# A transformer kernel of six blocks: attention products of two chunks interleaved, first feed-forward reordered, ring of 6 state buffers, relu(k) from PSUM

## The reference

```python
def _L0_attn_ref(...):        # stage 0, first half: linear attention, 16 heads
    qp, kp = elu(q) + 1, elu(k) + 1
    kv = einsum('bhsd,bhse->bhde', kp, v)
    z = einsum('bhsd,bhd->bhs', qp, kp.sum(axis=2))[..., None]
    attn = einsum('bhsd,bhde->bhse', qp, kv) / (z + EPS)
def _L0_xattn_ref(...):       # stage 0, second half: selective scan, 16 states, gated by z = x
    dA = exp(d[..., None] * A)
    state = state * dA + (d * u)[..., None] * b[:, None, :]
    y = einsum('bdn,bn->bd', state, c)
def _L0_ffn_ref(x, w_fc, w_proj):             # stage 1, inner width 1280
    # ternarize_weight: q in {-1, 0, 1} by a threshold of 0.7 * mean(|w|), times mean(|w|)
    h = square(relu(x @ ternarize_weight(w_fc).T))
    return h @ ternarize_weight(w_proj).T
def _L1_attn_ref(x, weight_qkv, weight_proj): # stage 2: causal, over the 4 batch entries
    qkv = x.reshape(-1, hidden) @ weight_qkv.T    # 16 query heads, 4 key/value heads of 32
    probs = softmax(where(causal, q @ k.T * scale, -inf))
    return (probs @ v) @ weight_proj.T
# stage 3: cross-attention, 16 heads of 128; stage 4: gated feed-forward with looked-up weights
x = layernorm(x + block(x))                   # after each of the six blocks
```

## Time and profile before

| | us |
|---|---|
| median of 3 runs (lowest, highest) | 3073.07 (3070.09, 3076.58) |
| profiled execution, its own time | 3069.51 |
| its span | 3067.8 |
| stage 0 in the span | 0 to about 880 |
| preparing stage 1 | about 880 to 909 |
| stage 1 | about 909 to 1107 |
| stage 2 | about 1117 to 1328 |
| stages 3 and 4 | the rest |

### The profile page before, as it was taken

The page is one execution under the profiler, slowest core; times in us unless marked ns, Lnnn a source line. Parts: engine busy times, 40 slices in busy tenths (PEclk is TensorE's granted clock), DMA queues, the critical chain, the costliest instruction groups (busy, mean ns, idle before and its releaser), DMA issues.

```text
span 3067.8 us, 29404 instructions
## 1 busy us (share of the span) xinstructions
PE 2742.9 (89%) x8882; PEld 1498.7 (49%) x8882; DVE 2002.3 (65%) x3924; ACT 1104.3 (36%) x2014; POOL 643.8 (21%) x569
## 2 busy tenths in 40 slices
PE   6788888788748877889999999999999999899998
PEld 2323333333326654445554555455544555478886
DVE  3996987988974436568782888278855788233222
ACT  4335335344322311135541555145532555221111
POOL 0542543525510024521111111011101111000000
PEclk9998998998979989999999999999999999999999
DMA  3111111101120121310002000200012001400000
GB/s 116 55 48 49 55 49 55 61 35 63 48 110 28 41 75 46 140 36 15 18 26 81 15 18 18 82 26 14 18 43 64 18 15 39 160 28 28 28 14 14
DMA packets 67391, 145.10 MB, mean 47 GB/s; under 512 B 8115, under 2 KB 24755, under 8 KB 66230
## 3 DMA queue, kind: packets, MB, share of 16 engines
q1 hardware_dynamic: 56310, 106.15, 10.6%
q0 software_dynamic: 5472, 21.01, 1.8%
q10 hardware_dynamic: 5472, 16.32, 1.5%
HBM read 113.77 MB, written 29.69 MB: 47 GB/s over the span
## 4 chain that ended last, share of the span: by engine, by line
PE 57%; DVE 25%; issue 10%; POOL 3%; ACT 2%; DMA 2%; DVEq 1%; SPq 1%; POOLq 0%; ACTq 0%
PE bank L474 32%; DVE h L1156 8%; PE bank L758 7%; PE bank L713 3%; PE bank L772 3%; PE bank L773 3%; PE bank L776 3%; DVE sm L1388 2%; DVE p L1399 1%; DVE val L1327 1%; PE bank L801 1%; PE bank L698 1%; PE bank L802 1%; PE bank L803 1%; DVE val L1335 1%
## 5 line engine op out<-in xcount | busy, mean ns | idle before, releaser
L1465 POOL TENSOR_TENSOR h<-du,Bb 128x1024 f32<-128x1024 f32 x128 | 308.7, 2418 | 220.9 <-DVE h L1161 131.5
L883 ACT ACTIVATE bank<-dt,A 128x512 f32<-128x512 f32 x256 | 176.8, 691 | 379.9 <-DVE h L1156 379.8
L1156 DVE TENSOR_TENSOR_SCAN h<-bank,h 128x512 f32<-128x512 f32 x256 | 297.8, 1203 | 15.3 <-POOL h L1465 15.1
L1005 ACT ACTIVATE p<-bank,sm,rq 128x512 f32<-128x512 f32 x256 | 199.0, 777 | 208.1 <-DVE sm L1392 208.1
L594 PE MATMUL bank<-h,ident 128*128 128x512 f32 x256 | 155.2, 690 | 100.7 <-DVE h L1161 100.6
L474 PE MATMUL bank<-pT,v 128*128 128x512 f32 x512 | 232.9, 598 | 3.1 <-ACT pT L828 3.1
L191 POOL TENSOR_SCALAR rstd<-mv 128x1 f32<-128x1 f32 x96 | 28.4, 295 | 981.3 <-DVE mv L185 981.3
L474 PE MATMUL bank<-xT,wxq 128*128 128x512 f32 x512 | 230.6, 593 | 3.2 <-ACT xT L828 3.2
L758 PE MATMUL bank<-woh,oT 128*128 128x512 f32 x512 | 224.4, 600 | 8.6 <-DMA woh<-in_Wo 6.6
L1520 POOL TENSOR_TENSOR rq<-rq,mhalf 128x4 f32<-128x4 f32 x64 | 65.5, 1024 | 790.8 <-DVE rq L1379 790.8
L474 PE MATMUL bank<-kr,q 128*128 128x512 f32 x512 | 230.6, 593 | 0.0
(11 more groups left out here) (199 smaller groups left out, 5085.0 us busy)
## 6 DMA issues: line engine op xcount, KB each, us to landing
Bb<-bc_dram SPq DMA_DIRECT2D x32, 512.0 KB, 3.6
Cb<-bc_dram SPq DMA_DIRECT2D x32, 512.0 KB, 3.8
x_dram<-xo POOLq DMA_DIRECT2D x16, 1024.0 KB, 4.7
xc<-x_dram SPq DMA_DIRECT2D x16, 1024.0 KB, 5.2
woh<-in_Wo SPq DMA_DIRECT2D x64, 256.0 KB, 2.7
idx<-in_idx SPq DMA_DIRECT2D x64, 129.0 KB, 2.1
w_dram<-val SPq DMA_DIRECT2D x64, 129.0 KB, 2.4
xc<-in_x SPq DMA_DIRECT2D x4, 1024.0 KB, 7.9
```

The costliest lines, as they stand in the source:

```text
L883: act.activation(bank[2 + n][:, :], dt[:, et, :], ACT.Exp, scale=A[:, et, 2 * w + n:2 * w + n + 1]).then_inc(dA_ready, 1)
L1005: act.activation(p4[:, t, :], bank[4 + t][:, :], ACT.Exp, bias=sm4[:, 4 + t:5 + t], scale=rq[:, hh % 2, 1, t:t + 1], accum_out=sm4[:, 8 + ...
L1156: dve.tensor_tensor_scan(h[:, s, n, :], bank[2 + n][:, :], h[:, s, n, :], 0.0, ALU.mult, ALU.add).then_inc(scanned, 1)
L1465: pool.tensor_tensor(h[:, U % HR, :, :], du[:, et:et + 1, :].to_broadcast([P, 2, S]), Bb[:, w % 2, :, :], ALU.mult).then_inc(dBu_ready, 1)
```

## The change

- `HR` goes from 4 to 6, so `input_of(U)` waits for PE's addition of unit U - 6 and, as before, for DVE's unit U - 3.
- relu(k) is no longer made by ACT: `exp_min` has two activations, and DVE takes max(k, 0) from the PSUM bank in the same instruction that adds the exponential. So PE may write over a key's bank only after DVE has read it (`key_consumed`), which stands ahead of keys 2 and 3 and of values 0 and 1.
- Stage 1: SP loads `w1` late in stage 0 and `w2` and x of chunk 0 as soon as their places are free; ACT sums both weights; x of chunk 0 is turned ahead of that and split between DVE's two halves of `q1`; PE starts with `q1` alone. In the loop, x of the next chunk is turned between the inner products and those down, and split ahead of the norms; the products down wait for the hidden tiles one by one.
- Stage 2: `qkv` has two buffers. While chunk c is attended, PE turns x of chunk c + 1 and makes its q, k, v between the output products; the orders of ACT, DVE and POOL are interleaved to match, with the norms of chunk c between the scores of chunk c + 1.
- The loops of stages 1 and 2 are written out on PE, ACT, DVE and SP, and stage 2's on POOL too.

```diff
-HR = 4
+HR = 6
-        qkv = s3("qkv", [P, B, QKV])
+        qkv = s3("qkv", [P, 2, B, QKV])
...
             if stages >= 2:
-                sp.wait_ge(stored, STORED0 + 16 * B)
-                simple_stage(1, rows_of)
+                sp.wait_ge(a_full, START + A0[0] + after(B - 1, PER_A[0], 24))
+                sp.dma_start(w1[:], io["w_fc"]...).then_inc(fc_loaded, 16)
+                sp.wait_ge(ln_sum, START + after(B, 8, -4))
+                weights(1, w2, io["w_proj"])
+                for c in range(B):
+                    load_chunk(1, c, c % 2, rows_of)
...
+                    def key_consumed(j):
+                        pe.wait_ge(qk_ready, START + after(c, KD + NT, KD + j + 1))
...
                         if U in (0, 1):
+                            key_consumed(U)
                             project(wk, U + 2, 16, 0)
+                        if U in (3, 4):
+                            key_consumed(U - 1)
                         if U in (3, 4, 6, 7):
                             project(wv, (U - 3) // 3 * 2 + U % 3, 20, 1)
...
+                pe.wait_ge(ln_sum, START + T0[1])
+                turn1(0)
                 pe.wait_ge(abs_sum, START + 2)
                 group(bank[6][:, 0:2], [(ones[:, :], am[:, 0, 0:2])], abs_all)
-                pe.wait_ge(tern, START + 2)
-                        turn(1, c, 0, xc[:, p], x_loaded[p], x_count(1, i))
-                        pe.wait_ge(x_split, START + after(c, KD, KD))
...
-                        pe.wait_ge(h_ready, START + after(c, KF0, KF0))
+                pe.wait_ge(tern, START + 1)
+                for c in range(B):
+                    inner(c)
+                    if c + 1 < B:
+                        turn1(c + 1)
+                    if c == 0:
+                        pe.wait_ge(tern, START + 2)
+                    down1(c)
...
+                turn2(0)
+                for b in range(B):
+                    project2(0, b)
+                for c in range(B):
+                    turn_attended(c, 0)
+                    if c + 1 < B:
+                        turn2(c + 1)
+                    out2(c, 0)
+                    for b in range(1, B):
+                        turn_attended(c, b)
+                        if c + 1 < B:
+                            project2(c + 1, b - 1)
+                        out2(c, b)
+                    if c + 1 < B:
+                        project2(c + 1, B - 1)
...
+                    def exp_min(j, k):
+                        d = filled(0, c, k)
+                        act.activation(er[:, j % 2, 0, :], d[:, :], ACT.Relu, scale=-1.0).then_inc(neg_ready, 1)
+                        act.activation(er[:, j % 2, 0, :], er[:, j % 2, 0, :], ACT.Exp, scale=-1.0).then_inc(a_done, 1)
...
+                act.wait_ge(fc_loaded, START + 16)
+                act.activation(wabs[:, :], w1..., ACT.Abs, accum_out=am[:, 0, 0:1]).then_inc(abs_sum, 1)
...
+                for c in range(B):                      # ACT, stage 2
+                    turned(c, 0)
+                    if c + 1 < B:
+                        x_turned(c + 1)
+                    turned(c, 1)
+                    exps(c, 3)
+                    if c + 1 < B:
+                        projected(c + 1, 0)
+                    turned(c, 2)
...
+                            dve.scalar_tensor_tensor(kp[:, j - KD, :], bank[j % 2][:, :], 0.0, er[:, j % 2, 0, :],
+                                                     ALU.max, ALU.add).then_inc(qk_ready, 1)
...
+                        attend(c, 2)                    # DVE, stage 2, for each c
+                        scores(c, 3)
+                        first(0)
+                        attend(c, 3)
                         dve.wait_ge(stored, STORED0 + 32 * B + 16 * c)
+                        last(0)
+                        scores(c + 1, 0)                # these only if c + 1 < B
+                        first(1)
+                        attend(c + 1, 0)
+                        last(1)
+                        scores(c + 1, 1)
+                        first(2)
+                        attend(c + 1, 1)
+                        last(2)
+                        scores(c + 1, 2)
+                        first(3)
+                        last(3)
```

More of the change, by code:

```diff
@@ L605, in _, with turn1, inner, down1 @@
             if stages >= 2:
+                def turn1(c):
+                    turn(1, c, 0, xc[:, c % 2], x_loaded[c % 2], x_count(1, c // 2))
+                def inner(c):
+                    pe.wait_ge(x_split, START + after(c, KD, KD))
+                    for f in range(KF0):
+                        d = a_bank(1, c, 4 + f)
+                        group(d[:, :], [(q1[:, k, f * P:(f + 1) * P], x[:, k, :]) for k in range(KD) for x in (x_hi, x_lo)], a_full)
+                def down1(c):
+                    for t in range(NT):
+                        pe.wait_ge(ln_sum, START + T0[1] + after(c, 4, t + 1 - 4))
+                        for f in range(KF0):
+                            if t == 0:
+                                pe.wait_ge(h_ready, START + after(c, KF0, f + 1))
+                            pe.matmul(bank[4 + t][:, :], h_hi[:, f, t * P:(t + 1) * P], q2[:, f, :], start=(f == 0), stop=False)
+                            m = pe.matmul(bank[4 + t][:, :], h_lo[:, f, t * P:(t + 1) * P], q2[:, f, :], start=False, stop=(f == KF0 - 1))
+                        m.then_inc(v_full, 1)
@@ new lines, in filled3, with x_turned, projected @@
+                def filled3(*name):
+                    return filled(2, 0, TILES3[name])
+                def x_turned(c):
+                    for k in range(KD):
+                        d = filled3("x", c, k)
+                        bring(xT[:, k, :], d[:, :])
+                def projected(c, b):
+                    if c >= 2 and b == 0:
+                        act.wait_ge(at_first, START + after(c - 1, B, 0))
+                        act.wait_ge(at_added, START + after(c - 1, ADDS, 0))
+                    for n in range(2):
+                        d = filled3("qkv", c, b, n)
+                        bring(qkv[:, c % 2, b, n * QKV // 2:(n + 1) * QKV // 2], d[:, 0:QKV // 2])
@@ new lines, in exps, with turned @@
+                def exps(c, b):
+                    s = sce[:, b * H0:(b + 1) * H0, 0:b + 1]
+                    act.wait_ge(sm_sub, START + after(c, B, b + 1))
+                    act.activation(s, s, ACT.Exp, scale=float(HD) ** -0.5).then_inc(sm_exp, 1)
+                def turned(c, b):
+                    d = filled3("at", c, b)
+                    bring(at3T[:, :, b * P:(b + 1) * P], d[:, :].rearrange("p (k s) -> p k s", k=KD))
+                x_turned(0)
+                act.wait_ge(ln_sum, START + T0[2])
@@ L1207, in _, with x_rest @@
             if stages >= 2:
-                dve.wait_ge(stage_loaded[1], START + L0[1])
-                dve.tensor_reduce(am[:, 0, 0:1], w1[:, :, :].rearrange("p k n -> p (k n)"), AX.X, ALU.add,
-                                  apply_absolute_value=True).then_inc(abs_sum, 1)
+                def x_rest(c):
+                    for k in range(KD):
+                        dve.wait_ge(a_done, START + A0[1] + after(c, PER_A[1], k + 1))
+                        dve.tensor_tensor(x_lo[:, k, :], bank[k][:, :], x_hi[:, k, :], ALU.subtract).then_inc(x_split, 1)
                 dve.wait_ge(abs_all, START + 1)
@@ L1249, in _, with scores @@
                 dve.wait_ge(stage_loaded[2], START + L0[2])
-                with dve.Fori(0, B // 2) as i:
-                    for p in range(2):
-                        c = 2 * i + p
-                        def scores(b):
+                for c in range(B):
+                    for p in (c % 2,):
+                        def scores(c, b):
                             s = sc[:, b * H0:(b + 1) * H0, 0:b + 1]
```

277 lines of the change are left out of this document (153 added, 124 removed).

## The result

The kernel after the change takes 3002.69 us by the median of its runs (2997.80 to 3006.79). The kernel before, timed beside it, takes 3074.82. The ratio is 0.9764, with a 95% interval of 0.9744 to 0.9783: 72 us are gone.

A forecast was written before the change was run, and what follows sets the result against it. Bounds: stage 0 mostly DVE, with a PE backlog; preparation weights' load and DVE; stage 1 PE; stage 2 three engines, none full. 0 - 15.4 - 34.9 - 25 = -75.3 from 3069.5 gives 2994.2 profiled, forecast 2996; range 2970 to 3018.

The forecast's parts named there:

- Stage 0, 0 predicted: Stage 0: at most 40 us of collisions could go, but the new key wait takes most back; net 0, bounds +8 and -40.
- the backlog: Stage 0, units 0 to 10: PE lags behind, so value tiles come late and POOL, held by PE's additions, meets DVE's multiplications.
- Whatever the ring does: Stage 0: DVE's unit 11 starts at 553.7 against 554.97, a gain of 1.3 us a chunk regardless of the ring.
- The loss at U = 30: Stage 0: with six slots POOL starts 2 us earlier and meets DVE's multiplication; about 1.1 us lost.
- Its price for relu(k) from PSUM: Stage 0, keys' additions: 0.74 us with a bank against 0.69, 0.8 us in all, hidden under PE's backlog.
- Preparing stage 1, -15.4 predicted: Before stage 1: earlier weight loads let PE start at 894.0 instead of 909.4; bounds -10 and -18.
- Stage 1, -34.9 predicted: Stage 1: 193.4 us falls to 158.5 as waits and six cold starts go; bounds -28 and -37.
- Stage 2, -25 predicted: Stage 2: last output product at T = 177 instead of 202, T counted from 1121.70; bounds -9 and -36.
- x is never late: Rival, stage 2: DVE runs ahead, so PE never waits for x; 10 us more gained, 2986; chance 0.10.
- DVE and POOL bound stage 2: Rival: port collisions keep the period at 46, stage 2 gives 9 us, 3012; chance 0.18 together with no early loads.
- The ring does what it looks made for: Rival, stage 0: POOL falls in step with DVE, up to 40 us of collisions go; at three quarters 2966; chance 0.13.
- Slower: Rival, stage 0: the wait for key 0 starves the scan; decides from 19 us a chunk; chance 0.01.

The follow-up runs named there:

- e2: Kernel after the change with the ring back at 4, so stage 0 keeps only relu(k) from PSUM with its wait; ratio 0.9800.
- e3: Kernel after the change with the ring back at 4 and relu(k) made by ACT again, without the wait; 3002.1 us, ratio 0.9753.
- e1: Kernel after the change with relu(k) made by ACT again, without the wait for the keys; the ring of 6 stays; ratio 0.9692.
- e7: Kernel after the change, but PE waits for both weights before stage 1's first inner product; 3009.73 us, ratio 0.9788.
- e4: Kernel after the change, but DVE reads key 0 ahead of unit 0 and key 1 ahead of unit 1; 2982.5 us, ratio 0.9693.
- e8: e4 with PE's loop of stage 0 written out besides; 2977.6 us, ratio 0.9687.
- e6: Kernel after the change with a third buffer of x, used in stage 2 only; ratio 0.9763.

## Why the prediction was right

It said 2996 us and 2970 to 3018; 3002.69 was measured, 6.7 more.

- **Stage 0, 0 predicted, +2.6.** The account up to unit 11 held to 0.8 us, and so did the conclusion that the backlog takes back what the ring gives. Two of its sentences were wrong. "Whatever the ring does" is refuted by e2: without the ring the same edit costs 19.5 us, because POOL is then held by PE's additions. And the collisions did not stay at 3.1 to 3.3 (which "units 7 to 13" overstates: only units 7, 8 and 10 had them). They shrank to 1.5 to 1.9, and the time became a wait for ACT. The loss at U = 30, put at 1.1 us, was 0.5: units 24 to 31 of chunk 2 took 35.9 us, before 35.4. Not foreseen at all was the jump of PE's loop. Chunk 1 to chunk 2, `wq` product to `wq` product, took 215.7 us against 212.5, though chunk 1's part of it, up to its last sum, was 2.0 shorter; the jump's 5.2 us are the whole 2.6 and more. That 0 came so near is in part luck: a gain of some 2.6 and a loss of 5.2, neither in the sum.
- **Its price for relu(k) from PSUM** (0.74 for 0.69 us) was 0.68. The keys' additions are no longer blocked, as predicted (19.6 us in e3, 10.9 after). But that needs no PSUM: e1, with the ring of 6 and both inputs in SBUF, has 10.9 too, and so has e2 with a bank and the ring of 4.
- **Preparing stage 1, -15.4 predicted, -16.8.** The steps stand, and e7 shows the one that was only argued: the second weight's 8.5 us lie under the inner products.
- **Stage 1, -34.9 predicted, -35.7.** No gap over 0.87 us.
- **Stage 2, -25 predicted, -21.4.** 2.5 us of the difference is the first run of 64 products, 23.45 us where the earlier trace rows had 20.92: the granted clock was 0.50 in its first 5 us and 1.00 there before, with 14.07 and 14.50 us of idle PE ahead of the turning. In e1, e4 and e8, with the same stage 2 and 20.9 us at the start, T is 176.8 to 176.9 where the sum had 177. The steps fit too: DVE's fourth sum of chunk 0 at T = 62.3 in e1 (62 predicted), the end of chunk 2's norms at 151.5 (151.4), stalls of 9.05 and 2.37 us (7 and 2.7). What failed is what the stall was said to cost. The sum has two chains to T = 151, PE's with its stalls (151.6) and DVE's (151.4), and counts the end from DVE's; yet the rival "x is never late" books 10 us for taking the stall out of PE's alone. e6 took 11.4 us of waits for x away and the rest came 0.7 us sooner, inside the spread. That the forecast of T came out is owed to DVE's chain: e6 ends where it ends with the loads' waits gone.
- **The rivals.** "x is never late" gives 0.7 us at most and not 10. "DVE and POOL bound stage 2" is right about who sets the pace, but the period is 42 to 43 us and not 46, near the 41 of the prediction's own sum. "The ring does what it looks made for" is real in e1, at 26.8 us, and was undone by the other half of the same change. "Slower" was near in kind: with the ring of 4 the wait for the keys costs 3.5 us in a chunk that has no jump ahead of it (e2 against e3).

## What to carry to other kernels

Two edits whose sum is nothing may be a gain and a loss of the same size: time them apart, since here the ring was worth 27 us and the place of two short instructions in VectorE's order cost 21 of them. Before a stall on one engine is booked as time to be won, add up the cycle of the next engine; the wait of 9 us for x was worth less than 1, because VectorE, waiting for GpSimd alone, needed 42 to 43 us a chunk. The read that frees another engine's buffer belongs in the reader's first idle moment and not behind its next long instruction.

## What was not expected of the hardware

- A VectorE multiplication with both inputs in SBUF took 5.52 us instead of 0.69, with four of GpSimd's products beside it that followed each other without a gap; the wait spans several instructions of the other engine.
- The jump back of TensorE's loop showed 2.6 to 3.2 us of idle TensorE in the eight kernels whose loop body had the waits for the keys, and none in the three without; written out, it was gone. In e4 the granted clock was 0.50 in the 5.1 us behind it.
- The first 48 products of stage 2 took 15.76 us in eight of the thirteen kernels profiled after the change and 18.1 to 18.3 us in the other five. The granted clock in the first 5 us was 1.00 in the eight and 0.50 to 0.52 in the five, which accounts for the difference. The idle TensorE ahead of the turning of x, 14.05 to 14.4 us in the eight and 13.9 to 14.1 in the five, does not tell them apart. Which it is changes T by 2.5 us, more than most edits to the stage did.
